# First stage: POOL instead of VectorE normalises the incoming group

## The reference

```
x = x + tanh(g_xattn[0]) * xattn0(layernorm(x), ctx)          # ctx: 32 x 77 x 128
x = x + tanh(g_ffn[0])   * moe0(layernorm(x))                 # 8 experts, top 2
x = x + tanh(g_xattn[1]) * xattn1(layernorm(x), ctx, mask)    # 16 heads
x = x + tanh(g_ffn[1])   * moe1(layernorm(x))                 # 8 experts, top 2, and a shared one

def layernorm(x): return (x - mean(x)) / sqrt(var(x) + 1e-5)  # over the 128 features
def xattn0(x1, x2):
    q, k, v = x1 @ w_q.T, x2 @ w_k.T, x2 @ w_v.T
    return softmax(q @ k.T / sqrt(128)) @ v
```

## Time and profile before

| | |
|---|---|
| Median of 3 runs | 727.38 us (726.87 to 729.06) |
| Profiled execution, its time | 728.11 us |
| Profiled execution, span of the trace | 726.1 us |
| Granted clock of TensorE, mean | 0.924 |
| Busy: PE, DVE, ACT, POOL | 88%, 77%, 59%, 14% |

### The profile page before, as it was taken

One profiled execution on the slowest core, in us unless ns is written; L12 is line 12 of the kernel. 1 busy time (PEld: TensorE's weight loads), 2 busy tenths in 40 slices (PEclk: granted clock), 3 DMA queues, 4 the chain that ended last, 5 costly groups with the idle time before them and its releaser, 6 DMA issues.

```text
span 726.1 us, 12574 instructions
## 1 busy us (share of the span) xinstructions
PE 635.6 (88%) x4078; PEld 498.2 (69%) x4078; DVE 561.4 (77%) x1267; ACT 426.9 (59%) x665; POOL 103.0 (14%) x127
## 2 busy tenths in 40 slices
PE   4765765999999999998599999999997499999996
PEld 3644654787787778776477767777775368888884
DVE  3877766798898889878578787777876588888885
ACT  3342331677777777775287777776675145555553
POOL 3444330020000000000500122022112100000000
PEclk9787565899999999999699999999998599999999
DMA  5323000000000000010244223422300000000000
GB/s 164 110 73 104 23 10 0 1 0 1 2 0 0 0 0 0 0 43 31 70 110 126 80 76 99 128 67 70 104 2 1 1 0 2 16 27 14 14 15 29
DMA packets 23705, 29.34 MB, mean 40 GB/s; under 512 B 3313, under 2 KB 17522, under 8 KB 23666
## 3 DMA queue, kind: packets, MB, share of 16 engines
q1 hardware_dynamic: 23666, 28.84, 13.9%
HBM read 19.99 MB, written 8.85 MB: 40 GB/s over the span
## 4 chain that ended last, share of the span: by engine, by line
PE 67%; DVE 17%; issue 6%; ACT 4%; POOL 2%; DMA 2%; SPq 1%; DVEq 0%; POOLq 0%; ACTq 0%
PE psum L397 13%; PE psum L399 12%; PE psum L398 12%; PE psum L1252 5%; PE psum L1267 3%; DVE c_mx L1423 2%; DVE c_sm L1429 2%; PE psum L1242 2%; PE psum L345 2%; DVE xn L326 2%; PE psum L919 2%; PE psum L1573 2%; PE psum L1243 2%; PE psum L537 2%; POOL rstd L319 1%
## 5 line engine op out<-in xcount | busy, mean ns | idle before, releaser
L397 PE MATMUL psum<-xh,w_hi 128*128 (+1 forms) x248 | 103.0, 415 | 2.2 <-DVE d_hr L1661 1.8
L1364 ACT ACTIVATE c_pt<-psum 77x512 f32<-77x512 f32 x128 | 74.8, 586 | 44.8 <-PE psum L1252 44.7
L398 PE MATMUL psum<-xl,w_hi 128*128 (+1 forms) x248 | 99.4, 401 | 0.0
L399 PE MATMUL psum<-xh,w_lo 128*128 (+1 forms) x248 | 99.2, 400 | 0.0
L869 DVE TENSOR_TENSOR b_hl<-b_hs,b_hh 128x1024 fp32r<-128x1024 f32 x64 | 78.2, 1222 | 15.5 <-ACT b_hh L863 15.5
L985 ACT ACTIVATE b_hr<-psum,b1s 128x512 f32<-128x512 f32 x128 | 81.0, 686 | 15.6 <-PE psum L399 15.5
L1045 DVE TENSOR_TENSOR b_hs<-b_hr,psum 128x1024 f32<-128x1024 f32 x64 | 77.8, 1215 | 15.3 <-ACT b_hr L985 13.8
L863 ACT ACTIVATE b_hh<-b_hs 128x1024 fp32r<-128x1024 f32 x64 | 67.9, 1061 | 33.1 <-PE psum L399 33.0
L1252 PE MATMUL psum<-ident,c_pf 128*77 128x128 f32 x512 | 74.4, 282 | 0.1
L1252 PEld LDWEIGHTS psum<-ident,c_pf 128*77 128x77 f32 x512 | 58.1, 149 | 14.4 <-issue 10.6
L1423 DVE TENSOR_REDUCE c_mx<-psum 128x8 f32<-128x616 f32 x64 | 50.9, 796 | 18.9 <-PE psum L1243 18.7
(11 more groups left out here) (209 smaller groups left out, 1271.9 us busy)
## 6 DMA issues: line engine op xcount, KB each, us to landing
w_hi<-c_q_spread SPq DMA_DIRECT2D x24, 256.0 KB
stage<-in_weights SPq DMA_DIRECT2D x8, 576.0 KB, 5.1
c_q_spread<-w_hi SPq DMA_DIRECT2D x7, 512.0 KB, 3.5
ctxg<-in_ctxT SPq DMA_DIRECT2D x16, 156.0 KB, 4.3
c_k_spread<-w_lo SPq DMA_DIRECT2D x8, 312.0 KB, 2.2
x_all<-in_x SPq DMA_DIRECT2D x8, 256.0 KB, 2.8
out_dram<-x_all SPq DMA_DIRECT2D x8, 256.0 KB, 2.3
c_kb<-c_k_spread SPq DMA_DIRECT2D x48, 39.0 KB
```

What stands on the lines that cost most here:

```text
L397: pe.matmul(o, wh, h, start=start, stop=False)
L398: pe.matmul(o, wh, l, start=False, stop=False)
L399: return pe.matmul(o, wl, h, start=False, stop=stop)
L1364: a_.activation(pt[:, q % NC4, :], bank[2 + q % 2][0:S2, :], ACT.Copy).then_inc(pt_done, 1)
```

## The change

The norm of the incoming group (`ln0`) is taken from DVE's program and put into POOL's, behind that group's rstd and ahead of its share of the weights' split. The wait for the transposes of two groups earlier, which guards the buffer of `xn0`, goes with it. The norm of `ln1` stays on DVE.

```diff
@@ pool_a
                 if a:
                     ln0.pool_rstd(q, a)
+                    if not (a.i is None and a.c < 2):
+                        q.wait_ge(ln0.t_ready, a.at(1, -1))
+                    ln0.pool_norm(q, a)
                     pool_split(q, a)
@@ dve_a
-                if a:
-                    if not (a.i is None and a.c < 2):
-                        v.wait_ge(ln0.t_ready, a.at(1, -1))
-                    ln0.dve_norm(v, a)
                 if m:
                     p = m.parity
```

## The result

The changed kernel takes 719.84 us, the median of 4 runs (717.47 to 721.19), against 728.22 for the kernel before in the same comparison (726.87 to 729.99). The ratio is 0.9869, 95% interval 0.984 to 0.9898: 1.3% faster, 8.4 us. The forecast was 720.9, that is 6.5 less than the 727.38 known then. The profiled execution, with a span of 715.7 us, was the fastest of the four.

What follows compares the result with a forecast made beforehand. The first stage's step cycle was taken as the bound, its norm held 2.28 us by POOL's split. Terms -6.1 + 0.25 - 0.7 = -6.5 gave 721.6 us from the profiled 728.11, 720.9 by the median 727.38; range 716.5 to 724.4.

Steps and rivals of the forecast that it cites:

- The norm was held by the split: First stage: DVE's norm waits 2.28 us for POOL's running w_lo split through the shared port, without a semaphore.
- Five times 1.2 us of distance: Groups 3 to 7, rstd's start to ln0's transposes: 3.34 us instead of about 4.54, saving 6.1 us in all.
- The head, +0.25: First three steps: POOL's longer norm, mostly hidden or offset by a freed a_rg, costs 0.25 us, between -0.3 and 3.3.
- a_rg slips in between POOL's two instructions: Loop steps: DVE's a_rg goes before POOL's subtraction or in the pair's 0.15 us gap, pushing POOL by perhaps 0.2.
- rival C: Loop steps: a_rg is held to the split's end, saving only 0.6 us a step, 724.6 us; chance 0.10.
- The clock, -0.7: First-stage loop: with less TensorE idle, one long low-clock stretch becomes short or less, worth -0.7 us.
- Rival B: Loop steps: TensorE's clock stays at 2.4 GHz in several, 1.4 us each; with three of five 717.4 us; chance 0.15.
- The rule that spoke against the change: Skill's warning that moving work between GpSimd and DVE might not help; by it a_rg is held through all POOL does.

Runs made afterwards that it cites:

- e3: The kernel before, with POOL's split made to wait for DVE's norm of the incoming group, nothing moved off DVE; 720.54 us, ratio 0.9873.
- e4: The kernel before, with POOL's split waiting for DVE's norm and for a_rg of the group before it; 715.17 us, ratio 0.9803.
- e2: The change for groups 3 to 7 alone, groups 0 to 2 keeping DVE's norm as in the kernel before; 721.04 us, ratio 0.9882.
- e9: The kernel before, with useless filler transposes on TensorE (3, 6 and 4 in a step); 725.43 us, ratio 0.9959.
- e6: The changed kernel, with useless filler transposes on TensorE (3, 6 and 4 in a step); 706.17 us, ratio 0.9686.
- e1: The change for groups 0 to 2 alone, groups 3 to 7 keeping DVE's norm as in the kernel before; 728.15 us, ratio 0.9996.
- e10: The kernel of e3 (split waits for DVE's norm but not for a_rg), with filler transposes on TensorE (3 and 6); 718.46 us, ratio 0.9841.
- e8: The changed kernel measured again, unaltered, on another occasion; 722.5 us, ratio 0.991 against the kernel before.

## Why the prediction was right

**The norm was held by the split: shown.** e3 and e4 move nothing off DVE and restore the 1.1 us norm; e3 alone gives the change's gain.

**Five times 1.2 us of distance: shown. That each is a step shorter by 1.2: not.** In the profile the distance is 3.34 for group 3 and 3.29 for the others, against 4.61 and 4.54 in the earlier trace rows: 1.27 and four times 1.24, 6.2. e2, with the change in these five groups alone, holds all of the gain by its median. At the full clock a step gives what the distance says (12.13 in e9, 10.77 in e6). Where both kernels are partly at the low clock, steps of like clock gained less than the 1.24: 0.84 (14.25 to 13.41, clock 0.76 and 0.75) and 0.96 (14.51 to 13.55, 0.65 and 0.62). There TensorE's own work is about to take over: it is not free before rstd + 3.08 (e3, e4). The prediction treated the norm as the bound in every step and did not ask where that ends; it ends 0.2 us below the 3.29, so the 6.1 holds by a small margin.

**The head, +0.25: right within what can be told.** e1 gives 0.9996. That the freed a_rg and the longer norm cancel there, as predicted, is not shown: a_rg falls from 2.18 to 0.23 in e1, but it does so in e2 as well, with the head of the kernel before.

**a_rg slips in between POOL's two instructions: shown.** It takes 1.10, and rival C did not come. C's mechanism is real where POOL has one long instruction: 2.2 us in e3 and e10. Its price was worked out too high: a held a_rg ends 0.02 after the split (in rows of the kernel before, 18.92 plus 2.18 against 18.46 plus 2.62), and not 0.23, so the router product would have begun at rstd + 7.2, not 7.5.

**The clock, -0.7: the term that was mis-sized.** In the two profiles ln0's last transposes move from 101.57 to 91.78, by 9.8 us. Distance is 6.2 of it, the head 1.5 (38.24 to 36.76, the scatter that e1 speaks of), and the remaining 2.1 lie in the steps from group 3 on, mostly in the first, which took 11.18 at a clock of 0.85. The same account for e8 gives 2.3 for the steps and a head that is 3.9 later (42.10), and for the long execution in e2's profile 1.0 lost in the steps and a head 4.6 later. So the steps' part ran from -2.3 to +1.0 and the head's from -1.5 to +4.6, where I had -0.7 and +0.25. The measured gain of 8.4 us in one comparison and 5.7 in the other holds the forecast 6.5 between them; that it fits to 1 or 2 us is in part luck. What I had not seen is how much clock was to be had: 16 us in e6 against e8. Rival B's 1.4 us a step makes 7, which is what the four steps gave (51.4 to 44.4); 5.7 more came ahead of group 3's rstd.

**The rule that spoke against the change** ("Perfetto Trace Analysis", section "Optimizing Scalar/DVE Operations", of the Trainium skill: moving work between the two engines that share a port might not help) did not decide here. DVE held by POOL, which it warns of, was the trouble before the change, and moving the norm put the short instructions ahead of the long one. e3 and e4 do that without moving it. By "SBUF — State Buffer", section "Who interferes with whom", of the Trainium skill, whichever issues first takes the shared ports and the other waits for its end. For the end the trace agrees: a_rg is through at 50.02, the subtraction ended at 49.99. Which of the two was first it does not show: a_rg's record begins at 48.92, 0.03 before the subtraction's.

## What to carry to other kernels

When a short DVE instruction on the critical path shows unexplained "issue" time, look at what POOL is running at that time, and first try to order the long instruction behind the short ones with a wait; behind the norm alone that was worth as much as moving the work (720.5 against 719.8 and 722.5), behind both short ones more (715.2). Then read what TensorE's clock does in the idle stretches that are left: cheap work there gave 15 to 16 us more on each of two orders (722.5 to 706.2, 715.2 to 700.3). It gave only 2 to 3 us on the two orders in which a held DVE instruction still kept TensorE waiting (728.6 to 725.4, 720.5 to 718.5), so it pays to remove the stalls first. Before trusting a difference of a few us between two profiles, profile the same kernel twice.

## What the runs showed of the hardware that was not expected

- Idle time of TensorE seems to cost more than itself. The same 13 filler transposes a step were worth 3 us with 2.08 us of idle left ahead of ln0's transposes (e9) and 16 us with 0.83 left (e6).
- Not every POOL instruction holds DVE. In the changed kernel the four instructions of ln1's norm run at 47.21 and take 1.08 in all, beside rstd on POOL from 47.94 to 48.98; behind a running split four of the same shape took 3.33.
- The same program puts one instruction of the first 40 us at places 5 us apart in two executions (30.53 and 36.01 for the first product), and e4's runs reach from 707.96 to 718.42.
- The granted clock in the profile can read 1.00 where durations are those of the low level: in e2 the windows from 0 to 20 and 20 to 40 us both give 1.00, and the four transposes at 33.41 take 1.06 us, as four in e3 at 66.86 do, where the clock reads 0.50. At the high level they take 0.66. In the first 40 us durations are the better witness.

```profile
20.00:40.00 20.00, 17.35 (x68) 14.76 (x69) 11.38 (x49) 6.96 (x12) 9.05 (x8) 1.00 0.33 97
```

```profile
33.41 1.06 PE L345 MATMUL psum<-ident,xn 128*128 128x128 f32 x4
```
